# Weight pieces in an attention and expert kernel: spread over sixteen groups, with low parts made on VectorE

## The chip, the cores and the metric

The kernel runs on one core of one Trainium2 chip. A core has a matrix engine (TensorE, PE in the profile, with its weight loads as PEld), a vector engine (VectorE, DVE), an activation engine (ScalarE, ACT), GpSimd (POOL) and SyncE (SP), which here only starts DMAs. Each engine works through its own list of instructions in order and waits on semaphores that others raise. The metric is the time of one execution in microseconds (us), as the median of several runs.

## The reference

```python
def reference(x, wq, bq, wk, bk, wv, bv, wo, bo, Ws, bs, Wg, Wu, Wd):   # x: (8, 512, 256) float16
    # attention: 16 heads of 16, causal, on the normalised rows
    n = layernorm(x)
    q, k, v = (n @ wq.T + bq) * 0.25, n @ wk.T + bk, n @ wv.T + bv      # split into heads
    attn = softmax(q k^T + causal mask).astype(float16)
    x = x + layernorm((attn v) @ wo.T + bo)
    # experts: 8 of them, 688 wide, the two best for each row
    n = layernorm(x)
    top, idx = top_k(n @ Ws + bs, 2);  combine = one_hot(idx) * softmax(top)
    h = silu(n Wg[e]) * (n Wu[e]);     y = h Wd[e]                      # Wg, Wu, Wd in float32
    return x + layernorm(sum over e of combine[e] * y[e])
```

## The kernel before

The attention part walks over 8 batches, and in each over 4 groups of 4 heads: 32 groups, numbered 0 to 31 (a group's number modulo 4 is its place in its batch, g). A group is 12 fills (i = 0 to 11). In each fill TensorE computes a block of transposed scores of this group (L1417) and, beside it in other rows of the array, a block of plain scores of the group after next (L1408). VectorE takes the row maxima of the plain ones (`maxima`, L1035), ScalarE exponentiates the transposed ones (L894, which writes pT), and GpSimd zeroes what lies above the diagonal (`cut`, an affine select, L681). TensorE then multiplies with the values (L1448). TensorE may start the scores of fill i when ScalarE has exponentiated up to fill i-2, and the plain scores of fill i when VectorE has taken the maxima up to fill i-2, since each has two banks. All other work is placed by hand at a fill: projections, the norms (`next_norm` for the next batch at g = 0, `finish` for the batch before at g = 1 and 2), the routing of rows (`route`, `slots` at g = 3) and the scatter of rows for the experts. The norm's root is GpSimd's: `rsqrt` is four small instructions, two of them powers of about 1 us each.

From group 18 on (FIRST_TILE) tiles of the expert part are woven into the groups; a later part (from about 712 us) does the other tiles and a last norm.

The expert weights are float32 in memory and are used as two float16 parts. There are 24 pieces (8 experts, Wg, Wd and Wu of each; n % 3 == 1 is Wd). A piece n is loaded by SyncE into one of two stages (`load_piece`), when the low part of piece n-2 is done, which frees its stage. Then, before the change:

- `high_part(n)` on ScalarE (L820): high = float16(256 * stage),
- `scale_stage(n)` on ScalarE (L826): stage = 256 * stage, in place,
- `low_part(n)` on GpSimd (L668): low = stage - high.

Pieces 0 to 5 (EARLY = 6) go through ahead of group 0; after them each of groups 0 to 8 has two (PIECES_AT), at fills 3 and 4 and at fills 7 and 8 of ScalarE's order and behind the first and second `cut` of GpSimd's.

At the start GpSimd writes all constants (L615 to L650) and raises const_ready, and only then comes `rsqrt(0)`, on which the first normalised rows `xn` wait. TensorE waits for const_ready ahead of its first transposition, VectorE ahead of its first bias of the values. SyncE clears the 8 MB of `expert_rows` with one DMA at the end of batch 2's list (L564). The pieces' DMAs and all others of SyncE are issued in the order of its code, each behind the waits of those ahead of it.

## Time and profile before

| | us |
|---|---|
| median of 3 runs (lowest, highest) | 924.04 (924.03, 924.41) |
| the profiled execution, its own time | 925.53 |
| its span, first to last instruction | 923.4 |
| groups 0 to 31 of the attention part | 49.42 to 620.53 |
| busy: PE, DVE, ACT, POOL | 769.0, 629.2, 556.9, 471.1 |
| mean granted TensorE clock | 0.79 |

The profile is of one execution. In a table of stretches the numbers are the stretch, its length, and for each engine its busy time in it with the count of its instructions, then the granted clock of TensorE (1.00 is 2.4 GHz, 0.50 is 1.2 GHz), the share of the DMA engines and the rate. In a timeline a row is the start, the duration, the engine, the line, the operation, what it writes and reads, and in brackets how long the engine had been idle and what released it. Group boundaries are taken at the first exponential (L894) of each group.

### The profile page before, as it was taken

To read this page: it belongs to the slowest core of one execution; us is meant where nothing else is said; L and a number is where in the kernel's file an instruction comes from. 1 tells how busy PE (TensorE), PEld (TensorE's weight loads), DVE (VectorE), ACT (ScalarE), POOL (GpSimd) and SP (SyncE) were. 2 spreads that over 40 slices of the span, in tenths; PEclk is the share of its full clock that TensorE was granted. 3 is DMA by queue.
4 is the path that set the end of the run, shared out by engine and by line. 5 is a ranking of instruction groups with operands and counts; after the bars stand their busy time and mean duration, and the time that the engine had idled before them with its cause. 6 is when DMAs were issued, how large, how long until landed. Compare 5 with 4: busy or idle time off the path is not lost. (4 is left out here: it accounts for less than half of the span.)

```text
span 923.4 us, 21865 instructions
## 1 busy us (share of the span) xinstructions
PE 769.0 (83%) x6606; PEld 447.4 (48%) x6607; DVE 629.2 (68%) x2328; ACT 556.9 (60%) x1101; POOL 471.1 (51%) x540
## 2 busy tenths in 40 slices
PE   3568886789999999988998899898977999999930
PEld 1122232333333335554554455466865878778720
DVE  3855668778877787888889787755644555555546
ACT  3589887675666567665676577555543444444427
POOL 3575647475352445675366447757544223333227
PEclk9555555555555569998999899899997999999975
DMA  5343323315601011122111212212333532323248
GB/s 173 126 121 98 120 77 112 91 38 187 223 24 30 25 41 16 22 48 53 19 30 31 41 19 43 53 25 45 56 73 84 110 41 40 46 34 47 34 104 283
DMA packets 69243, 66.52 MB, mean 72 GB/s; under 512 B 5536, under 2 KB 62752, under 8 KB 69152
## 3 DMA queue, kind: packets, MB, share of 16 engines
q1 hardware_dynamic: 55872, 50.86, 17.9%
q0 software_dynamic: 13280, 14.49, 11.2%
q8 instruction: 51, 0.84, 0.4%
q14 instruction: 40, 0.33, 0.1%
HBM read 34.04 MB, written 31.29 MB: 71 GB/s over the span
## 5 line engine op out<-in xcount | busy, mean ns | idle before, releaser
L1035 DVE CUSTOM_DVE_ANT_0 unused<-bank,mask 128x384 f16<-128x384 f32 (+3 forms) x512 | 235.9, 485 | 83.8 <-PE bank L1408 80.7
L894 ACT ACTIVATE pT<-bank 128x512 f16<-128x512 f32 (+1 forms) x384 | 201.7, 533 | 108.9 <-PE bank L1417 105.8
L1417 PE MATMUL bank<-qT,kT 32*128 32x384 f16 (+3 forms) x512 | 176.3, 390 | 29.3 <-ACT pT L894 27.4
L1408 PE MATMUL bank<-kT,qT 32*128 32x384 f16 (+3 forms) x512 | 178.6, 398 | 8.2 <-DVE nmax L1035 7.7
L681 POOL TENSOR_SCALAR_AFFINE_SELECT pT<-pT 128x512 f16<-128x512 f16 x128 | 84.7, 706 | 129.1 <-ACT pT L894 128.4
L1837 POOL DMA_INDIRECT expert_rows<-y_sb,dest x36 | 56.0, 1555 | 118.8 <-DVE y_sb L1956 113.3
L1510 PE MATMUL bank<-tile_xT,gu_part 128*128 128x256 f16 (+1 forms) x616 | 90.0, 287 | 11.7 <-DVE stage L1219 11.6
L2031 PE MATMUL bank<-xT,gu_part 128*128 128x256 f16 (+1 forms) x792 | 94.7, 277 | 2.4 <-issue 1.4
L1417 PEld LDWEIGHTS bank<-qT,kT 32*128 32x128 f16 x512 | 39.5, 97 | 117.3 <-issue 60.6
L1448 PEld LDWEIGHTS bank<-va,pT 128*128 128x128 f16 x1280 | 49.4, 102 | 91.6 <-issue 66.7
L2031 PEld LDWEIGHTS bank<-xT,gu_part 128*128 (+1 forms) x792 | 77.9, 101 | 18.0 <-issue 3.7
L1448 PE MATMUL bank<-va,pT 128*128 128x17 f16 x1280 | 70.1, 176 | 15.5 <-POOL pT L681 15.3
L160 POOL DMA_INDIRECT dispatch_rows<-rows,slot x64 | 65.3, 1021 | 21.3 <-issue 16.6
L2056 PE MATMUL bank<-wd_part,h 128*128 (+2 forms) x612 | 75.4, 273 | 0.6 <-ACT h L1878 0.3
L1510 PEld LDWEIGHTS bank<-tile_xT,gu_part 128*128 (+1 forms) x616 | 58.2, 103 | 28.1 <-issue 17.6
L1528 PE MATMUL bank<-wd_part,stage 128*128 (+2 forms) x476 | 70.7, 283 | 0.3 <-DVE stage L1225 0.3
L707 POOL DMA_INDIRECT expert_rows<-tile_y,tile_dest x34 | 54.8, 1613 | 26.1 <-ACT tile_y L879 19.9
L1871 ACT ACTIVATE act_g<-bank 128x512 f32<-128x512 f32 (+1 forms) x72 | 32.5, 477 | 55.2 <-PE bank L2031 55.2
L668 POOL TENSOR_TENSOR gu_part<-stage,gu_part 128x1280 f16<-128x1280 f32 (+1 forms) x32 | 47.0, 1488 | 35.5 <-ACT stage L826 35.5
L2056 PEld LDWEIGHTS bank<-wd_part,h 128*128 128x128 f16 (+2 forms) x612 | 54.0, 97 | 17.5 <-issue 10.9
L1878 ACT ACTIVATE h<-hid 128x512 f16<-128x512 f32 (+1 forms) x72 | 37.7, 523 | 40.9 <-DVE hid L1936 40.2
L1936 DVE SCALAR_TENSOR_TENSOR hid<-bank,act_g 128x512 f32<-128x512 f32 (+1 forms) x72 | 39.9, 554 | 31.3 <-ACT act_g L1871 30.7
(198 smaller groups left out, 1439.7 us busy)
## 6 DMA issues: line engine op xcount, KB each, us to landing
expert_rows<-tile_in SPq DMA_DIRECT2D x1, 8192.0 KB, 26.5
stage<-wg SPq DMA_DIRECT2D x8, 688.0 KB, 4.1
stage<-wu SPq DMA_DIRECT2D x8, 688.0 KB, 4.1
stage<-wd SPq DMA_DIRECT2D x8, 640.0 KB, 4.1
gu_part<-expert_rows SPq DMA_DIRECT2D x16, 256.0 KB, 6.5
out<-gu_part SPq DMA_DIRECT2D x16, 256.0 KB, 2.5
tile_in<-dispatch_rows SPq DMA_DIRECT2D x21, 130.0 KB
rows<-dispatch_rows SPq DMA_DIRECT2D x18, 130.0 KB
```

The lines of the kernel that those rows point to most:

```text
L160: gp.indirect_dma_start(out=xs_dram[:, :], in_=keep["rows"][:, t, r, :], in_offset=None, out_offset=bass.IndirectOffsetOnAxis(ap=keep["slo ...
L681: last = gp.affine_select(out=diagonal, in_=diagonal, compare_op=ALU.is_ge, fill=0.0, base=0, pattern=[[0, J], [1, P]], channel_multiplier=-1)
L894: sc.activation(pT[:, lo:hi], ST_BANK[i % 2][:, 0:hi - lo], ACT.Exp, scale=1.0 / INV_SCALE).then_inc(p_ready, 1)
L1035: last = v.tensor_tensor_reduce(out=unused[:, i % 2, at:at + n], in0=S_BANK[i % 2][:, at:at + n], in1=mask[:, T - n:T], scale=-1.0, scalar ...
L1408: last = mm(S_BANK[i % 2][:, at:at + n], qT[32 * j:32 * j + 32, g, P * qt:P * (qt + 1)], kT[32 * j:32 * j + 32, g, 0:n], start=True, stop= ...
L1417: last = mm(ST_BANK[i % 2][:, at:at + n], kT[32 * j:32 * j + 32, g, P * kt:P * (kt + 1)], qT[32 * j:32 * j + 32, g, P * kt:T], start=True, ...
L1448: last = mm(OUT[:, qt, j, 0:HD + 1], pT[:, at:at + P], va[:, g, kt, j, :], start=(i == 0 and qt == 0), stop=(i == NF - 1 and qt == QT - 1))
L1510: last = mm(target, keep["gu"][part][:, bass.ds(col + (k * GU + at), width_)], tile_xT[n % 2][:, k, :], start=(s == 0), stop=(s == 2 * KD ...
L1528: last = mm(Y_BANK[:, D * t:D * (t + 1)], h[0:rows, c // 2, at:at + P], keep["wd"][w][0:rows, bass.ds(col + c * D, D)], start=(c == 0 and ...
L1837: gp.indirect_dma_start(out=ys_dram[:, :], in_=y_sb[j][:, t, :], in_offset=None, out_offset=bass.IndirectOffsetOnAxis(ap=dest[j][:, t:t + ...
L2031: last = mm(dst[0:width, :], gu_part[part][:, bass.ds(col + (k * GU + at), width)], xT[j][:, k, :], start=(s == 0), stop=(s == 2 * KD - 1))
L2056: last = mm(Y_BANK[t][:, 0:D], h[0:rows, c // 2, at:at + P], wd_part[w][0:rows, bass.ds(col + c * D, D)], start=(c == 0 and s == 0), stop= ...
```

## The change

It does six things.

1. EARLY is 5: pieces 0 to 4 go through ahead of group 0. Groups 0 to 3 have two pieces each, groups 4 to 13 and group 15 one each (group 14 none): PIECES_OF.
2. Pieces 0 to 4 and the first piece of each of groups 0 to 3 keep the old way (POOLED, nine pieces). The other 15 have no `scale_stage` and no `low_part` on GpSimd. VectorE makes their low part straight from the unscaled stage, low = 256 * stage - high, as a scalar_tensor_tensor in two halves (`low_half`): at fills 10 and 11 in groups 0 to 3, later at the fills of LOW_AT. The high part is at fill 7 in groups 0 to 3, later at HIGH_AT.
3. The semaphore lo_ready becomes two, pool_low and dve_low, and a load waits for the one that its stage's last piece raises.
4. GpSimd's constants are put in another order: what `rsqrt(0)` and the first transposition need comes first, then `rsqrt(0)`, then the rest and const_ready. TensorE waits for the new ident_ready ahead of the transposition, and for const_ready ahead of its first projection.
5. The clear of `expert_rows` is eight DMAs, one in each of groups 8 to 15 of SyncE's list. The first tile's load and store wait for all eight.
6. SyncE's loads of pieces are spread like the pieces: each group's list holds the loads of its pieces' successors but one.

```diff
-        EARLY = 6
-        PIECES_AT = {(b, g): tuple(range(EARLY + 2 * (G * b + g), min(EARLY + 2 * (G * b + g) + 2, PIECES)))
-                     for b in range(B) for g in range(G)}
+        EARLY = 5
+        PIECES_OF = [2] * G + [1] * (2 * G) + [1, 1, 0, 1]
+        LAST_PIECES = len(PIECES_OF)
...
+        POOLED = tuple(range(EARLY)) + tuple(PIECES_AT[0, g][0] for g in range(G))
+        LOW_RANK = [sum((m in POOLED) == (n in POOLED) for m in range(n)) for n in range(PIECES)]
+        HIGH_AT = (6, 0, 5, 6)
+        LOW_AT = ((8, 9), (2, 3), (7, 8), (8, 9))
+        CLEARS = 2 * G
...
-                        sp.wait_ge(lo_ready, n - 1)
+                        sp.wait_ge(pool_low if n - 2 in POOLED else dve_low, LOW_RANK[n - 2] + 1)
...
+                    def pieces(g):
+                        for n in PIECES_AT[b, g]:
+                            if n + 2 < PIECES:
+                                load_piece(n + 2)
+
+                    def clear_rows(g):
+                        n = G * b + g - 2 * G
+                        if 0 <= n < CLEARS:
+                            rows = RESULTS // CLEARS
+                            sp.wait_ge(const_ready, 1)
+                            sp.dma_start(ys_dram[n * rows:(n + 1) * rows, :].rearrange("(n p) d -> p n d", p=P),
+                                         clear.unsqueeze(1).broadcast_to([P, rows // P, D])
+                                         ).then_inc(keep["cleared"], 16)
...
                 def low_part(n):
 
-                    pool.wait_ge(scaled_ready, n + 1)
+                    pool.wait_ge(scaled_ready, LOW_RANK[n] + 1)
...
-                            if c < len(PIECES_AT[b, g]):
-                                low_part(PIECES_AT[b, g][c])
+                            if first and c == 0:
+                                low_part(PIECES_AT[b, g][0])
...
-                            if i in (3, 7) and i // 4 < len(PIECES_AT[b, g]):
+                            if first and i in (3, 7):
                                 high_part(PIECES_AT[b, g][i // 4])
-                            if i in (4, 8) and i // 4 <= len(PIECES_AT[b, g]):
-                                scale_stage(PIECES_AT[b, g][i // 4 - 1])
+                            if first and i == 4:
+                                scale_stage(PIECES_AT[b, g][0])
+                            if not first and i == HIGH_AT[g]:
+                                for n in PIECES_AT[b, g]:
+                                    high_part(n)
...
+                def low_half(n, half):
+
+                    if half == 0:
+                        dve.wait_ge(hi_ready, n + 1)
+                    for (dst, src), (high, _) in zip(places(n, 1), places(n, 0)):
+                        if n % 3 == 1:
+                            cols = slice(half * FC * D // 2, (half + 1) * FC * D // 2)
+                            last = v.scalar_tensor_tensor(dst[:, cols], src[:, cols], WSCALE, high[:, cols], ALU.mult, ALU.subtract)
+                        else:
+                            last = v.scalar_tensor_tensor(dst[:, half, :], src[:, half, :], WSCALE, high[:, half, :],
+                                                          ALU.mult, ALU.subtract)
+                    if half:
+                        last.then_inc(dve_low, 1)
...
+                            if i in ((10, 11) if first else LOW_AT[g]):
+                                for m in PIECES_AT[b, g][1:] if first else PIECES_AT[b, g]:
+                                    low_half(m, i - (10 if first else LOW_AT[g][0]))
...
-                pe.wait_ge(const_ready, 1)
+                pe.wait_ge(ident_ready, 1)
                 pe.wait_ge(xn_ready, 1)
                 transpose4(("xnT", 0), xn, range(KD))
                 pe.wait_ge(w_in, 16 * 10)
+                pe.wait_ge(const_ready, 1)
```

**Place 1: GpSimd, from the constants to the first norm.** The rows give the line, the operation and the tile. Before:

```order
L632 IOTA iota_s 128x4
L634 MEMSET gu_part 128x16x16 x2
L636 MEMSET ident 128x128
L637 AFFINE_SELECT ident<-ident 128x128
L640 MEMSET before 128x128
L641 AFFINE_SELECT before<-before 128x128
L644 MEMSET mask 128x512
L646 AFFINE_SELECT mask<-mask 128x128
L649 MEMSET va 128x16 x4
L657 TENSOR_SCALAR veps<-mv 128x4
```

With the change:

```order
L656 MEMSET gu_part 128x16x16 x2
L658 MEMSET before 128x128
L659 AFFINE_SELECT before<-before 128x128
L634 TENSOR_SCALAR veps<-mv 128x4
L635 CAST mean<-mv 128x4
L637 TENSOR_TENSOR std<-veps,power 128x4
L639 TENSOR_TENSOR rstd<-std,power 128x4
L662 IOTA iota 128x8
L664 IOTA fill 128x8
L666 IOTA next 128x9
L668 MEMSET one_early 128x8
```

The norm's four instructions (veps to rstd) stand ahead of six small constants, the mask and the four columns of va; ident has moved ahead of spare_ids.

**Place 2: ScalarE, a group of batch 1.** L820 (L836 in the change) is `high_part`, L826 (L842) is `scale_stage`, L894 (L911) the exponentials. Before, from fill 3 on:

```order
L799 ACTIVATE qT<-bank,bq_sb 128x512
L820 ACTIVATE gu_part<-stage 128x2x640
L820 ACTIVATE gu_part<-stage 128x2x48
L894 ACTIVATE pT<-bank 128x512
L826 ACTIVATE stage<-stage 128x1376
L894 ACTIVATE pT<-bank 128x512
L802 ACTIVATE kT<-bank,bk_sb 128x512
L894 ACTIVATE pT<-bank 128x512 x2
L807 ACTIVATE v<-bank 128x256
L820 ACTIVATE wd_part<-stage 128x1536
L894 ACTIVATE pT<-bank 128x256
L809 ACTIVATE qT<-bank 128x512
```

With the change, the same stretch of group 4:

```order
L815 ACTIVATE qT<-bank,bq_sb 128x512
L911 ACTIVATE pT<-bank 128x512 x2
L818 ACTIVATE kT<-bank,bk_sb 128x512
L911 ACTIVATE pT<-bank 128x512
L836 ACTIVATE wd_part<-stage 128x1536
L911 ACTIVATE pT<-bank 128x512
L823 ACTIVATE v<-bank 128x256
L911 ACTIVATE pT<-bank 128x256
L825 ACTIVATE qT<-bank 128x512
```

One high part stands where two high parts and two scalings stood.

**Place 3: VectorE, the end of a group at g = 3 (group 11).** L1035 (L1055 in the change) is `maxima`, L1128 (L1148) and after it `slots`, L1257 is `low_half`. Before:

```order
L1035 ISA unused,nmax<-bank,mask 128x512
L1035 ISA nmax 128x1
L1025 TENSOR_TENSOR va<-v,bv_sb 128x16x16
L1035 ISA unused,nmax<-bank,mask 128x512
L1035 ISA nmax 128x1
L1035 ISA unused,nmax<-bank,mask 128x512
L1035 ISA nmax 128x1
L1128 TENSOR_TENSOR row<-bank,fill 128x32
```

With the change:

```order
L1055 ISA unused,nmax<-bank,mask 128x512
L1055 ISA nmax 128x1
L1257 SCALAR_TENSOR_TENSOR gu_part<-stage,gu_part 128x640
L1257 SCALAR_TENSOR_TENSOR gu_part<-stage,gu_part 128x48
L1045 TENSOR_TENSOR va<-v,bv_sb 128x16x16
L1055 ISA unused,nmax<-bank,mask 128x512
L1055 ISA nmax 128x1
L1257 SCALAR_TENSOR_TENSOR gu_part<-stage,gu_part 128x640
L1257 SCALAR_TENSOR_TENSOR gu_part<-stage,gu_part 128x48
L1055 ISA unused,nmax<-bank,mask 128x512
L1055 ISA nmax 128x1
L1148 TENSOR_TENSOR row<-bank,fill 128x32
```

The two halves of a low part stand behind the maxima of fills 8 and 9, ahead of `slots`.

## Rows read from the trace of the kernel before

**Rows 1.** The page's second part: granted TensorE clock in 40 equal slices.

```profile
PEclk9555555555555569998999899899997999999975
```

**Rows 2.** Table of stretches: groups 4 to 12.

```profile
109.64:126.97 17.33, 14.47 (x111) 5.80 (x112) 13.39 (x48) 14.44 (x25) 12.69 (x14) 0.50 0.28 87
126.97:143.57 16.60, 13.41 (x97) 4.75 (x94) 10.42 (x44) 13.74 (x25) 7.84 (x9) 0.50 0.33 102
143.57:164.56 20.99, 13.17 (x100) 4.95 (x100) 18.09 (x52) 12.77 (x21) 13.76 (x14) 0.50 0.33 100
164.56:180.61 16.05, 13.31 (x130) 5.28 (x131) 11.08 (x56) 14.33 (x25) 6.52 (x6) 0.50 0.27 88
180.61:200.04 19.43, 15.85 (x111) 6.08 (x112) 16.53 (x59) 14.61 (x23) 12.95 (x14) 0.50 0.17 50
200.04:213.37 13.33, 13.21 (x97) 4.74 (x94) 9.98 (x44) 8.96 (x20) 10.29 (x15) 0.50 0.10 32
213.37:228.23 14.86, 13.03 (x101) 5.14 (x100) 12.66 (x52) 8.12 (x17) 7.56 (x12) 0.50 0.67 223
228.23:241.51 13.28, 12.97 (x131) 5.28 (x130) 9.81 (x56) 9.74 (x20) 2.38 (x4) 0.50 1.05 348
241.51:258.19 16.68, 15.78 (x111) 6.07 (x111) 12.64 (x60) 9.86 (x19) 7.59 (x12) 0.50 0.29 95
```

**Rows 3.** Timeline, all engines: from GpSimd's constants to the first projection.

```profile
3.00 0.14 POOL L624 IOTA iota<- 128x8 f32 x1 [0.24 <-POOL ids L622]
...
4.80 0.31 POOL L634 MEMSET gu_part<- 128x256 f16 x1 [0.15 <-POOL iota_s L632]
...
5.67 0.38 DVE L1007 BATCH_NORM_AGGREGATE mv<-stats 128x2 f16<-128x6 f32 x4
...
7.50 0.53 POOL L644 MEMSET mask<- 128x512 f16 x1 [0.16 <-POOL before L641]
...
9.75 0.24 POOL L657 TENSOR_SCALAR veps<-mv 128x4 f16<-128x4 f16 x1
...
12.37 1.11 DVE L1015 TENSOR_SCALAR xn<-x_sb,mean,rstd 128x256 f16<-128x256 f16 x4 [6.32 <-POOL rstd L662]
...
15.91 1.01 PE L1390 MATMUL bank<-xnT,wq_sb 128*128 128x512 f16 x2 [1.27 <-ACT xnT L795]
```

**Rows 4.** Timeline of ScalarE: the last piece ahead of group 0.

```profile
46.70 1.43 ACT L820 ACTIVATE gu_part<-stage 128x1280 f16<-128x1280 f32 x2
...
49.42 1.07 ACT L894 ACTIVATE pT<-bank 128x512 f16<-128x512 f32 x2
```

**Rows 5.** Timelines of VectorE and GpSimd: three places where both work at once.

```profile
60.04 1.24 POOL L681 TENSOR_SCALAR_AFFINE_SELECT pT<-pT 128x512 f16<-128x512 f16 x2
...
60.72 0.70 DVE L1025 TENSOR_TENSOR va<-v,bv_sb 128x256 f16<-128x256 f16 x1
...
190.35 3.25 DVE L1015 TENSOR_SCALAR xn<-x_sb,mean,rstd 128x256 f16<-128x256 f16 x1
190.41 3.10 POOL L668 TENSOR_TENSOR wd_part<-stage,wd_part 128x1536 f16<-128x1536 f32 x1 [0.67 <-ACT stage L826]
...
222.04 1.04 POOL L660 TENSOR_TENSOR std<-veps,power 128x4 f16<-128x4 f16 x1
...
222.61 0.29 DVE L1025 TENSOR_TENSOR va<-v,bv_sb 128x256 f16<-128x256 f16 x1
```

**Rows 6.** Timeline of TensorE: two waits for ScalarE, in groups 0 and 2.

```profile
55.89 0.50 PE L1417 MATMUL bank<-qT,kT 32*128 32x384 f16 x1 [1.46 <-ACT pT L894]
...
93.25 0.39 PE L1417 MATMUL bank<-qT,kT 32*128 32x256 f16 x1 [1.08 <-ACT pT L894]
```

**Rows 7.** Groups by line and shape: VectorE's subtractions in the later part (count, busy us, mean ns).

```profile
L1943 DVE TENSOR_TENSOR h<-hid,h 128x512 f16<-128x512 f32 x36 | 25.2, 701 | 25.7 <-ACT h L1878 24.9 <-issue 0.8
...
L1943 DVE TENSOR_TENSOR h<-hid,h 128x256 f16<-128x256 f32 x18 | 7.7, 426 | 0.5
```

**Rows 8.** Table of stretches: from slots in group 11 to fill 6 of group 12.

```profile
241.10:250.20 9.10, 8.81 (x48) 2.58 (x46) 8.66 (x48) 5.15 (x9) 3.53 (x6) 0.50 0.43 142
```

79 lines of the change are left out of this document (41 added, 38 removed).

## The prediction

> **What bounds the kernel now.** I read the granted clock first, then a table of stretches cut at the groups, then timelines inside the groups, and last the prices by shape.
>
> TensorE runs at half its clock, 1.2 GHz, in 13 of the first 14 slices of the page and at about full clock afterwards [rows 1]. In that slow stretch two kinds of group stand side by side. Groups 9 to 12 have no weight piece: TensorE is busy in 13.21 of 13.33 us, 12.97 of 13.28, 15.78 of 16.68 [rows 2]. They are bound by TensorE at its low clock. Groups 4 to 8 have two pieces each and take 17.33, 16.60, 20.99, 16.05 and 19.43 us, though TensorE's work in them is the same within 0.3 us at the same place g, but for group 4 [rows 2]. Their idle TensorE time is 2.9, 3.2, 7.8, 2.7 and 3.6 us: that is what the pieces cost. Two mechanisms make it. First, ScalarE: its high parts and scalings stand between exponentials, and TensorE waits for those, as in the 1.46 us in group 0 and the 1.08 us in group 2 [rows 6]. The same 1.08 recurs in groups 1 and 3. Second, GpSimd's subtraction holds VectorE: a tensor_scalar of VectorE that began 0.06 us ahead of a 3.10 us subtraction took 3.25 us [rows 5] and ended with it. Behind it queue the row maxima, and behind those TensorE. From group 12 on nothing of the pieces is left in the trace. The end follows from there through the tiles, so time won in groups 0 to 16 is won in full, unless something new is late.
>
> **The start.** The moments of the first norm are ready at 6.05 (5.67 + 0.38), but GpSimd starts the root at 9.75, behind its constants [rows 3]. The change moves two stretches of constants behind it: 3.00 to 4.80, and 7.50 to 9.75, 4.05 us in all. The root can't start before the moments, and ids, which VectorE waits for in its first memsets, comes a little later (two more instructions ahead of it). So it starts at about 6.25, 3.5 us earlier. The first projection follows xn by 15.91 - 12.37 = 3.5 us [rows 3] and would start at about 12.4. But it now waits for const_ready. The root takes 2.5 us (9.75 to about 12.3), to 8.8, and the 4.05 us of constants behind it end at about 12.9. I take 2.9 us won; the ends are 0 (the pieces' loads don't follow) and 3.5.
>
> With EARLY = 5 the high part and scaling of piece 5 no longer stand ahead of the first exponential: 49.42 - 46.70 = 2.7 us [rows 4]. ScalarE is the last to arrive there, so all of it is won. Together **5.6 us**.
>
> **Groups 0 to 3.** Each keeps two high parts and one scaling on ScalarE and loses the scaling at fill 8. The 1.08 us wait behind that scaling [rows 6] goes, four times: 4.3. In group 0 piece 5's data is loaded earlier than piece 6's was, and most of the 1.46 goes: 1.2. Against it VectorE gets two halves at fills 10 and 11 in a stretch where it is idle about half the time; I take 0.7 for the four groups. One subtraction a group stays on GpSimd, and it will still meet the norm of group 0. **4.8 us** won.
>
> **Groups 4 to 8.** Without any piece I expect the busy time of TensorE in the group plus the idle time of the clean group at the same g: 14.47 + 0.9 = 15.4 for group 4, 13.5 for 5, 13.17 + 1.8 = 15.0 for 6, 13.6 for 7, and 16.7 for 8, the length of group 12 [rows 2]. That is 74.2 against 90.4 us: **16.2 us** won. One high part of about 1.4 us per group stays on ScalarE. It is free: ScalarE was idle in 3.5 to 6.8 us of the groups without pieces (13.28 - 9.74, 16.68 - 9.86) [rows 2], and GpSimd has no subtraction left there.
>
> **The price of the low parts on VectorE.** No such instruction is in the trace. The nearest is the float32 subtraction from SBUF: 426 ns for 256 columns and 701 for 512 [rows 7], so 1.07 ns a column and 0.15 fixed. A half of 640 + 48 columns occupies about 0.8 us, one of 768 about 0.9. 15 pieces make 24.8 us. The part on the path has the ends 0 and 24.8. VectorE is idle for 3.4, 2.2, 3.5 and 4.0 us in groups 9 to 12 [rows 2], more than 1.65 each time, so I take the value by what stands behind each place:
> - g = 3 (groups 7, 11; 15 likewise): two halves ahead of slots. From slots to fill 6 of the next group VectorE is busy 8.66 of 9.10 us [rows 8]. Only about 0.4 us of idle lies ahead, so 1.2 us go on to the next group, three times: 3.6.
> - g = 2 (groups 6, 10): they push the second norm's scaling at fills 9 and 10, which was itself waiting for the root: 0.5 each, 1.0.
> - g = 1 (groups 5, 9, 13): VectorE waits for TensorE at fills 0 to 3; 0.2, 0.2 and, with the plan behind it, 0.4: 0.8.
> - g = 0 (groups 4, 8, 12): the halves fall where VectorE is idle again: 0.
> - meetings with GpSimd's selects: a two-input add took 0.70 us beside a select, and 0.29 beside the root's power [rows 5]. So only the selects count, 0.4 to 0.6 a meeting. By their places few meet; I take 1.5 in all.
>
> **6.9 us** lost.
>
> Here a rule of the Trainium skill speaks against the change. Its page SBUF — State Buffer, section Who interferes with whom, says that a VectorE instruction with two SBUF inputs contends with a GpSimd instruction that reads SBUF, and whichever is second blocks until the first is done. `low_half` is such an instruction. For the select and the subtraction the trace agrees, for the power it does not. By the rule a half could be held by any GpSimd work beside it; that is the second rival.
>
> **The rest.** The clear in one piece filled the DMA engines in group 11 (share 1.05), and the group took the same 13.28 us that TensorE needs [rows 2]. Eight clears of an eighth cost nothing on this evidence, with or against; a late load would be their only harm, and each piece is now loaded over a group ahead. The two semaphores cost nothing.
>
> Sum: 5.6 + 4.8 + 16.2 - 6.9 = 19.7 us. The profiled execution took 925.53 and would take 905.8; it stands 1.5 above the median, so the median goes from 924.04 to **904.3**.
>
> **Rivals.**
> - *The start gives only the piece.* The loads of pieces 2 and 4 each wait for a low part of GpSimd and then for the transfer, and ScalarE waits for them ahead of group 0. If that chain doesn't shift with xn, 2.9 us are lost again: 907.2. Against it: each link of it begins with a release by ScalarE, whose work follows xn. 10%.
> - *Slower: VectorE and GpSimd hold each other.* If every one of the 30 halves meets a select of 0.62 us and nothing of the low parts is hidden, the price is 24.8 + 30 x 0.62 = 43.4 instead of 6.9 us, and the kernel takes 940.8. It decides from a price of 26.6 / 15 = 1.77 us a piece on the path, more than the whole instruction pair, so only with the meetings. For it: [rows 5]. Against: VectorE's idle time of 2.2 to 4.0 us a group, and the powers and scatters don't hold it. 3%.
> - *VectorE becomes the bound.* All 24.8 on the path, with few meetings: 904.3 + 17.9 = 922.2. It would need VectorE without idle time in each group. 5%.
> - *The clock rises earlier.* TensorE without its gaps in groups 4 to 8 could be granted full clock there. VectorE would then bound these groups at its busy 10 to 13 us plus the low parts, where I count 13.3 to 17.9: some 30 us more over 14 groups, about 874. Against it: groups 9 and 11 kept TensorE busy 98 to 99% and stayed at 0.50 [rows 2]. The skill's page TensorE: Matmul & The Clock Gate, Part 1, says that activity releases the throttle; by that alone the rise could come earlier, but these rows show a busy engine that isn't released. 4%.
>
> **How the numbers follow.** The forecast has 78%. Its bounds: the start 0 to 3.5, the low parts 3 to 14, groups 0 to 8 by 3 us either way, and the clock's changes after group 17, which may fall differently by 2 us or so. That gives 895 to 912, and it holds the first rival. With the other three at 12% that range should hold the time 8 times in 10. A measurement of this kernel can tell about 0.2%, 1.8 us, from no change. Faster by more: 96% (the forecast, the first and fourth rival and most of the third); within 0.2%: 1%; slower: 3%.
>
> **What would show it.** Right: the first xn at about 8.9 and the first exponential of group 0 near 43.8; groups 1 to 3 near 14; 4 to 7 at 15.4, 13.7, 15.5 and 13.6, and 8, 12 and 16 near 17.9; half of a Wg piece near 0.7 us for its 640 columns; the clock at 0.5 until about 8 us into group 18. Wrong: VectorE instructions of over 1.2 us beside selects; groups 9 to 16 each over a microsecond longer; waits of TensorE for row maxima in most fills; ScalarE waiting for stage loads after group 0; or a tile that waits for the clears in group 16.

## Result: 9.3 us faster, a little under half of what was forecast

| | before | changed |
|---|---|---|
| median of 4 runs on one chip, us | 924.22 (924.03 to 924.48) | 914.95 (913.95 to 915.81) |
| ratio | | 0.9896 (95%: 0.9869 to 0.9923) |
| profiled execution, its own time | 925.53 | 913.95 |
| its span | 923.4 | 912.2 |
| first exponential of group 0 | 49.42 | 44.16 |
| groups 0 to 17 | 283.78 | 275.84 |
| groups 18 to 31 | 287.34 | 291.91 |
| behind group 31 | 302.84 | 300.27 |

The forecast was 904.3 with a range up to 912. Between the two spans lie 11.2 us, against 19.7 forecast. Up to group 18 the profile shows 13.2; the groups behind it took 4.6 more and the later part 2.6 less. The medians are 9.3 us apart and not 11.6, as the two profiled times are, because the profiled execution stands 1.3 us above its median before the change and 1.0 below with it; no stage explains that part.

The ratios below leave out executions that took over 1.5% longer than the fastest of their kernel (912.95 and 1232.26 us with the halves in VectorE's gaps, 940.14 us with the small subtractions, 940.51 us of before), and the profiles of 912.95 and 940.14 us are used up to group 17 only, where the granted clock is 0.50 as in all traces.

The page of the changed kernel, granted TensorE clock in 40 slices, answers to [rows 1]. There too 13 of the first 14 slices are at half clock:

```profile
PEclk9555555555555579988998899799997999999975
```

The start, from the timeline of all engines, answers to [rows 3]. GpSimd's root no longer waits behind the constants, and xn comes 3.2 us earlier (12.37 to 9.15):

```profile
6.90 1.05 POOL L637 TENSOR_TENSOR std<-veps,power 128x4 f16<-128x4 f16 x1
...
9.15 1.11 DVE L1035 TENSOR_SCALAR xn<-x_sb,mean,rstd 128x256 f16<-128x256 f16 x4 [2.70 <-POOL rstd L639]
...
13.31 1.01 PE L1428 MATMUL bank<-xnT,wq_sb 128*128 128x512 f16 x2 [1.89 <-POOL va L676]
...
41.25 1.48 ACT L836 ACTIVATE wd_part<-stage 128x1536 f16<-128x1536 f32 x1 [5.71 <-DMA stage<-wd]
```

The table of stretches, groups 2 to 6, 8, 11 and 12 of the changed kernel (columns as in [rows 2]):

```profile
71.95:86.86 14.91, 13.07 (x92) 4.38 (x92) 10.19 (x40) 11.40 (x20) 5.64 (x7) 0.50 0.39 125
86.86:101.33 14.47, 13.02 (x93) 4.38 (x92) 9.79 (x38) 11.36 (x22) 5.79 (x7) 0.50 0.26 87
101.33:118.98 17.65, 15.85 (x111) 6.09 (x111) 14.27 (x55) 11.11 (x19) 5.19 (x9) 0.50 0.23 65
118.98:132.61 13.63, 13.63 (x96) 5.05 (x94) 11.90 (x48) 10.10 (x21) 4.57 (x8) 0.50 0.37 120
132.61:148.27 15.66, 13.00 (x100) 5.08 (x101) 14.26 (x56) 9.12 (x18) 5.97 (x9) 0.50 0.25 80
162.48:180.43 17.95, 16.43 (x113) 6.33 (x114) 14.30 (x69) 11.09 (x21) 7.62 (x11) 0.50 0.18 54
209.88:224.03 14.15, 13.39 (x125) 5.24 (x124) 11.23 (x54) 10.75 (x22) 3.30 (x4) 0.50 0.16 56
224.03:242.39 18.36, 16.42 (x113) 6.32 (x114) 14.69 (x69) 11.07 (x20) 7.48 (x11) 0.50 0.37 118
```

Groups 5, 6 and 8 are where the forecast put them (13.7, 15.5, 17.9). Group 4 is not: 17.65 us against 15.4. Nor are 2 and 3, forecast near 14. TensorE's idle time did fall in these, to 1.8, 1.5 and 1.8 us; but it is *busy* longer, 15.85 us in group 4 against 14.47 in [rows 2], with 111 instructions in both. The next section takes this apart.

### The profile page after: what moved, and what is told of

It is laid out like the page before. It is cut to its first block and busy times, and to the rows that moved or that the text cites. A ratio compares the mean times of both kernels' runs of the same rounds, so it can differ in the third digit from the quotient of the medians.

```text
span 912.2 us, 21884 instructions
## 1 busy us (share of the span) xinstructions
PE 778.4 (85%) x6606; PEld 451.9 (50%) x6607; DVE 640.6 (70%) x2378; ACT 538.2 (59%) x1086; POOL 435.6 (48%) x515
## 5 line engine op out<-in xcount | busy, mean ns | idle before, releaser
L1055 DVE CUSTOM_DVE_ANT_0 unused<-bank,mask 128x384 f16<-128x384 f32 (+3 forms) x512 | 235.2, 484 | 61.1 <-PE bank L1446 58.1
L911 ACT ACTIVATE pT<-bank 128x512 f16<-128x512 f32 (+1 forms) x384 | 202.0, 531 | 122.5 <-PE bank L1455 121.2
L1455 PE MATMUL bank<-qT,kT 32*128 32x384 f16 (+3 forms) x512 | 177.6, 393 | 14.1 <-ACT pT L911 13.0
L1446 PE MATMUL bank<-kT,qT 32*128 32x384 f16 (+3 forms) x512 | 179.0, 399 | 9.5 <-DVE nmax L1055 8.8
L698 POOL TENSOR_SCALAR_AFFINE_SELECT pT<-pT 128x512 f16<-128x512 f16 x128 | 88.3, 734 | 170.5 <-ACT pT L911 170.3
L1548 PE MATMUL bank<-tile_xT,gu_part 128*128 128x256 f16 (+1 forms) x616 | 94.0, 297 | 6.9 <-DVE stage L1239 6.6
L1455 PEld LDWEIGHTS bank<-qT,kT 32*128 32x128 f16 x512 | 39.5, 97 | 103.1 <-issue 60.2
L160 POOL DMA_INDIRECT dispatch_rows<-rows,slot x64 | 66.8, 1043 | 21.3 <-issue 16.7
L1566 PE MATMUL bank<-wd_part,stage 128*128 (+2 forms) x476 | 72.7, 289 | 0.0
L1548 PEld LDWEIGHTS bank<-tile_xT,gu_part 128*128 (+1 forms) x616 | 60.3, 107 | 22.7 <-issue 11.7
L1231 DVE SCALAR_TENSOR_TENSOR stage<-stage,bank 128x256 f32<-128x256 f32 x84 | 34.9, 416 | 39.7 <-ACT stage L869 38.8
L869 ACT ACTIVATE stage<-bank 128x256 f32<-128x256 f32 x84 | 32.2, 383 | 50.9 <-PE bank L1548 50.4
```

The costliest lines, as they stand in the source:

```text
L160: gp.indirect_dma_start(out=xs_dram[:, :], in_=keep["rows"][:, t, r, :], in_offset=None, out_offset=bass.IndirectOffsetOnAxis(ap=keep["slo ...
L698: last = gp.affine_select(out=diagonal, in_=diagonal, compare_op=ALU.is_ge, fill=0.0, base=0, pattern=[[0, J], [1, P]], channel_multiplier=-1)
L911: sc.activation(pT[:, lo:hi], ST_BANK[i % 2][:, 0:hi - lo], ACT.Exp, scale=1.0 / INV_SCALE).then_inc(p_ready, 1)
L1055: last = v.tensor_tensor_reduce(out=unused[:, i % 2, at:at + n], in0=S_BANK[i % 2][:, at:at + n], in1=mask[:, T - n:T], scale=-1.0, scalar ...
L1446: last = mm(S_BANK[i % 2][:, at:at + n], qT[32 * j:32 * j + 32, g, P * qt:P * (qt + 1)], kT[32 * j:32 * j + 32, g, 0:n], start=True, stop= ...
L1455: last = mm(ST_BANK[i % 2][:, at:at + n], kT[32 * j:32 * j + 32, g, P * kt:P * (kt + 1)], qT[32 * j:32 * j + 32, g, P * kt:T], start=True, ...
```

## Experiments

The chips of these runs differed: the kernel before took 931.21, 925.45, 932.45 and 933.03 us there, with runs from 922.3 to 940.5, where the forecast's chip had 924.22. So the times in microseconds that the expectations name, made for that chip, can't be held against these runs within some us: each kernel is compared by its ratio to before, and by the length of its groups 0 to 17 in the trace. That sum repeats well: 275.84, 275.76 and 275.92 us in three traces of the changed kernel, 283.78, 283.74 and 283.97 in three of before. Every row but the first keeps the changed kernel's start, with EARLY = 5 (the last has 4), and so has 19 pieces in groups 0 to 17 (the last 20), where before had 18.

| groups, us | 0-3 | 4-8 | 9-17 | 0-17 | ratio to before |
|---|---|---|---|---|---|
| before | 60.22 | 90.40 | 133.16 | 283.78 | 1 |
| changed | 57.17 | 79.10 | 139.57 | 275.84 | 0.990 |
| no halves | 54.64 | 74.71 | 133.80 | 263.15 | 0.971 |
| all lows on GpSimd | 59.10 | 82.54 | 144.85 | 286.48 | 0.999 |
| two a group | 57.19 | 92.04 | 135.03 | 284.26 | 0.994 |
| halves in gaps | 57.13 | 76.80 | 133.91 | 267.84 | 0.973 |
| first piece | 55.33 | 77.45 | 139.61 | 272.39 | 0.982 |
| both placements | 55.39 | 75.19 | 133.92 | 264.50 | 0.972 |
| both, EARLY = 4 | 60.08 | 75.17 | 134.41 | 269.66 | 0.968 |

### What the halves cost

```diff
-                        sp.wait_ge(pool_low if n - 2 in POOLED else dve_low, LOW_RANK[n - 2] + 1)
+                        if n - 2 in POOLED:
+                            sp.wait_ge(pool_low, LOW_RANK[n - 2] + 1)
+                        else:
+                            sp.wait_ge(hi_ready, n - 1)
...
+                            if n not in POOLED:
+                                sp.wait_ge(hi_ready, n + 1)
+                                for (dst, _), (high, _) in zip(places(n, 1), places(n, 0)):
+                                    sp.dma_start(dst, high).then_inc(dve_low, 16)
...
-                            if i in ((10, 11) if first else LOW_AT[g]):
-                                for m in PIECES_AT[b, g][1:] if first else PIECES_AT[b, g]:
-                                    low_half(m, i - (10 if first else LOW_AT[g][0]))
```

> The changed kernel without VectorE's halves; the 15 low parts are left out (a DMA puts a copy of the high part in their place). Theory A, the halves make the row maxima late and so pull TensorE's pairs of plain and transposed scores apart: groups 2, 3 and 4 become shorter by about 1.0, 1.0 and 1.7 us, groups 9 to 16 by the 6.4 us that they lost against the kernel before, the pairs overlap for 5.5 us a group again, and the kernel takes 901 to 903 us. Rival B, VectorE is late in groups 0 to 8 with or without the halves, once ScalarE no longer holds TensorE back: only groups 9 to 16 become shorter, 908 to 909 us. Rival C, the halves are hidden and the loss is made elsewhere: 914 to 916 us.

Measured: 902.46 us, ratio 0.9707 (0.9652 to 0.9761). Groups 0 to 17 take 263.15 us, 12.7 less than with the halves. Theory A holds, B and C fall. Groups 2, 3 and 4 became shorter by 1.41, 1.01 and 1.62 us. The edit also frees a stage at the high part, earlier than the changed kernel can. That this isn't the gain is shown by the run of both placements below: it makes every low part and takes 264.50 us over the same groups.

The timeline shows how a late VectorE costs time without a wait of TensorE that one would see. First the changed kernel, TensorE and VectorE at the start of group 3 (86.86): L1455 is the transposed scores, L1446 the plain ones, L1255 a half, L1055 the maxima.

```profile
85.88 0.95 DVE L1255 SCALAR_TENSOR_TENSOR wd_part<-stage,wd_part 128x768 f16<-128x768 f32 x1
86.22 0.60 PE L1455 MATMUL bank<-qT,kT 32*128 32x512 f16 x1
86.22 0.60 PE L1446 MATMUL bank<-kT,qT 32*128 32x384 f16 x2
86.75 0.68 DVE L1055 CUSTOM_DVE_ANT_0 unused<-bank,mask 128x512 f16<-128x512 f32 x1
86.97 0.60 PE L1455 MATMUL bank<-qT,kT 32*128 32x512 f16 x1
87.36 0.09 DVE L1055 DVE_READ_ACCUMULATOR2_ANT nmax<- 128x1 f16 x1
87.36 0.95 DVE L1255 SCALAR_TENSOR_TENSOR wd_part<-stage,wd_part 128x768 f16<-128x768 f32 x1
87.50 0.60 PE L1446 MATMUL bank<-kT,qT 32*128 32x384 f16 x2
```

Then the same place without the halves (L1460 transposed, L1451 plain, L1063 maxima):

```profile
85.07 0.60 PE L1460 MATMUL bank<-qT,kT 32*128 32x512 f16 x1
85.08 0.60 PE L1451 MATMUL bank<-kT,qT 32*128 32x384 f16 x2
...
85.82 0.60 PE L1460 MATMUL bank<-qT,kT 32*128 32x512 f16 x1
85.83 0.60 PE L1451 MATMUL bank<-kT,qT 32*128 32x384 f16 x2
85.86 0.56 DVE L1063 CUSTOM_DVE_ANT_0 unused<-bank,mask 128x384 f16<-128x384 f32 x1 [0.19 <-PE bank L1451]
```

The plain and the transposed scores work in different rows of the array and run side by side: both start at 86.22 and both take 0.60. With the half ahead of it the row maximum is read out at 87.36 only, and the next plain scores start at 87.50 where the transposed ones started at 86.97. The two now run one behind the other, 0.53 us lost, and TensorE shows as busy throughout. (The starts are recorded; the ends of matmuls are modelled by the profile.) That is why, from before to the changed kernel, TensorE's idle time in group 3 fell by 1.4 us (2.86 to 1.45) and the group's length only by 0.5: 0.9 went into busy time. In groups 2, 3 and 4 the two kinds overlap for 4.44, 4.49 and 3.88 us, against 5.49, 5.49 and 5.47 before and 5.49, 5.49 and 5.11 without the halves (the time in which both run, summed over the trace of the group).

The price by kind, VectorE's groups by shape in the changed kernel (count, busy us, mean ns):

```profile
L1257 DVE SCALAR_TENSOR_TENSOR gu_part<-stage,gu_part 128x640 f16<-128x640 f32 x20 | 17.8, 889 | 0.0
L1255 DVE SCALAR_TENSOR_TENSOR wd_part<-stage,wd_part 128x768 f16<-128x768 f32 x10 | 10.3, 1029 | 0.0
L1257 DVE SCALAR_TENSOR_TENSOR gu_part<-stage,gu_part 128x48 f16<-128x48 f32 x20 | 6.6, 329 | 0.0
```

That is 34.7 us, 2.3 a piece, where the forecast had 24.8. Of the 50 instructions, 38 were not held and took 0.95 us (768 columns), 0.82 (640) and 0.20 (48), which makes 29.9 us for all. The other 4.8 are holds: 12 instructions took 0.3 to 0.4 us longer, each beside a select of GpSimd. Here two instructions take 1.36 us from 124.07, beside a select that began at 124.00:

```profile
124.00 0.64 POOL L698 TENSOR_SCALAR_AFFINE_SELECT pT<-pT 128x512 f16<-128x512 f16 x1 [5.71 <-ACT pT L911]
124.07 1.36 DVE L1257 SCALAR_TENSOR_TENSOR gu_part<-stage,gu_part 128x640 f16<-128x640 f32 x2
```

Halves beside GpSimd's casts, powers and scatters were not held. It can be GpSimd that waits: the cast of the norm's mean, 0.18 us elsewhere, took 0.83 beside a half, while that half and the one beside the powers took, with their 48 columns, 0.94, as with nothing beside them:

```profile
141.06 0.94 DVE L1257 SCALAR_TENSOR_TENSOR gu_part<-stage,gu_part 128x640 f16<-128x640 f32 x2
141.10 0.83 POOL L635 CAST mean<-mv 128x4 f32<-128x4 f16 x1
141.90 1.04 POOL L637 TENSOR_TENSOR std<-veps,power 128x4 f16<-128x4 f16 x1
142.53 0.94 DVE L1257 SCALAR_TENSOR_TENSOR gu_part<-stage,gu_part 128x640 f16<-128x640 f32 x2
```

### Spreading and VectorE, one at a time

The first edit spreads the pieces but leaves every low part to GpSimd, the second gives the halves to VectorE but doesn't spread.

```diff
-        POOLED = tuple(range(EARLY)) + tuple(PIECES_AT[0, g][0] for g in range(G))
+        POOLED = tuple(range(PIECES))
...
-                            if first and c == 0:
-                                low_part(PIECES_AT[b, g][0])
+                            if first and c < 2:
+                                low_part(PIECES_AT[b, g][c])
+                            elif not first and c == 1:
+                                for n in PIECES_AT[b, g]:
+                                    low_part(n)
...
+                            if not first and i == HIGH_AT[g] + 1:
+                                for n in PIECES_AT[b, g]:
+                                    scale_stage(n)
```

> The spreading of the changed kernel alone: one piece a group from group 4 on, as before the change with a scaling on ScalarE and a subtraction on GpSimd. Theory A, the gain comes from taking the scaling and the GpSimd subtraction away, which cost about 1.6 us a piece (16.2 us for the ten pieces of groups 4 to 8): 15 pieces x 1.6 in place of about 13 us for the halves, so about 11 us slower than the changed kernel, 925 to 927 us. Rival, the spreading makes the gain, and one piece a group hides whichever engine does it: 905 to 915 us.

```diff
-        PIECES_OF = [2] * G + [1] * (2 * G) + [1, 1, 0, 1]
+        PIECES_OF = [2] * (2 * G + 1) + [1]
```

> VectorE's halves without the spreading: groups 4 to 8 have two pieces each and group 9 one, both pieces at the fills of the changed kernel. Theory A, a piece costs about 0.85 us wherever it is: groups 4 to 9 cost 4.7 us more than with one piece, groups 10 to 17 4.7 less, the sum of groups 0 to 17 is 275 to 277 and the kernel takes 914 to 916. Rival, two pieces are more than VectorE has idle time for in a group (4 us of halves against 1.5 to 4.5 us) and two high parts more than ScalarE's pace allows: groups 4 to 8 take 8 to 12 us more, the sum is 279 to 283 and the time 918 to 922.

Spreading alone: 928.36 us, ratio 0.9988 (0.9954 to 1.0021), groups 0 to 17 at 286.48, 2.7 more than before. VectorE alone: 925.76 us, ratio 0.9940 (0.9914 to 0.9965), 284.26 us, 0.5 more than before. Together they give 275.84. So theory A of the first run holds (10.6 us more than the changed kernel), and that of the second falls; its rival has the direction, but groups 4 to 8 took 12.9 us more, beyond its 8 to 12. Neither half of the change gains anything in these groups by itself, though both versions bring one piece more into them than before had; the two make 7.9 us together. With two pieces in a group the halves crowd, and ScalarE comes to wait for loads, as its waits in groups 4 to 8 show (us in total, times, longest):

```profile
ACT gu_part L836 <- DMA stage<-wg: 2.2, 1, 2.2
ACT wd_part L836 <- DMA stage<-wd: 2.0, 1, 2.0
```

How much of the 8.4 us is crowding and how much the fills, which were chosen for one piece, this run doesn't tell.

### How GpSimd holds VectorE

The run with all low parts on GpSimd, each subtraction cut into instructions of 128 columns.

```diff
-                        last = gp.tensor_tensor(dst, src, high, ALU.subtract)
+                        if n % 3 == 1:
+                            for c in range(0, FC * D, D // 2):
+                                last = gp.tensor_tensor(dst[:, c:c + D // 2], src[:, c:c + D // 2], high[:, c:c + D // 2], ALU.subtract)
+                        else:
+                            size = src.shape[-1]
+                            step = P if size > P else size
+                            for k in range(KD):
+                                for c in range(0, size, step):
+                                    last = gp.tensor_tensor(dst[:, k, c:c + step], src[:, k, c:c + step], high[:, k, c:c + step],
+                                                            ALU.subtract)
```

> The run with all low parts on GpSimd, one piece a group, with each subtraction cut into instructions of 128 columns instead of 640 to 1536 (some 12 a piece). Theory A, VectorE is held for the length of one GpSimd instruction: no VectorE instruction takes more than about 1 us beside them, group 6 goes from 19.25 to about 16.5 us and group 10 from 19.74 to about 16.5, in all 6 to 8 us less than with whole subtractions, 918 to 921 us. Rival, VectorE is held for the whole work however it is cut: groups 6 and 10 stay above 19 us and the time at 924 to 930.

Measured: 926.35 us, ratio 1.0002 (0.9978 to 1.0026); groups 6 and 10 take 18.86 and 18.91 us against 19.25 and 19.74, and groups 0 to 3 take 64.65 against 59.10. The mechanism of theory A is there, its gain is not: groups 4 to 17 take 4.2 us less than with whole subtractions, and groups 0 to 3 take 5.6 more. Timelines of group 10, first with whole subtractions:

```profile
212.27 3.65 DVE L1040 TENSOR_SCALAR rows<-y,mean,rstd 128x256 f16<-128x256 f16 x2
212.75 3.09 POOL L685 TENSOR_TENSOR wd_part<-stage,wd_part 128x1536 f16<-128x1536 f32 x1
```

and with small ones:

```profile
219.81 0.99 DVE L1049 TENSOR_SCALAR rows<-y,mean,rstd 128x256 f16<-128x256 f16 x2
220.29 4.66 POOL L687 TENSOR_TENSOR wd_part<-stage,wd_part 128x128 f16<-128x128 f32 x12
...
221.34 1.00 DVE L1049 TENSOR_SCALAR rows<-y,mean,rstd 128x256 f16<-128x256 f16 x2
```

Two scalings beside the subtraction took 3.65 us and take 0.99: VectorE waits for one instruction of GpSimd, not for its work. This is the lock that the Trainium skill describes on its page SBUF — State Buffer, section Who interferes with whom, held for a whole instruction, and the trace agrees. But the work grew from 3.09 us to 4.66, and from 2.93 to 4.36 for a Wg or Wu piece, and now the select behind it is late. TensorE waits for that in the same group:

```profile
205.05 4.36 POOL L693 TENSOR_TENSOR gu_part<-stage,gu_part 128x128 f16<-128x128 f32 x12
209.35 0.65 POOL L707 TENSOR_SCALAR_AFFINE_SELECT pT<-pT 128x512 f16<-128x512 f16 x1
...
210.06 0.27 PE L1496 MATMUL bank<-va,pT 128*128 128x17 f16 x4 [3.17 <-POOL pT L707]
```

### The start and the clears

```diff
-                pool.sem_inc(ident_ready, 1)
...
-                rsqrt(0)
...
                 last.then_inc(const_ready, 1)
+                rsqrt(0)
...
-                pe.wait_ge(ident_ready, 1)
```

(The cut lines move ident, gu_part and before behind iota_s again.)

> The changed kernel with GpSimd's constants and the first root in the order of before, and TensorE waiting for const_ready alone. Theory A: the first xn comes about 3 us later and the first exponential with it, at 46.7 to 47.0 instead of 44.16; 917.5 to 918.5 us. Rival, the loads of the pieces set the first exponential and don't follow xn: it stays at 44.2 and the time at 914 to 916.

Measured: 920.88 us, ratio 0.9897 (0.9867 to 0.9927). xn is 3.2 us later (12.36 against 9.15), the first exponential 2.1 us (46.28 against 44.16), groups 0 to 17 the same (275.88). So of the 5.3 us won at the start the constants make 2.1 and the rest, 3.1, is put down to the piece, which no run took away alone; a third of what xn gains doesn't reach the first exponential. The first exponential itself differs by 0.8 us between executions (43.8 to 44.6 in eleven traces whose code up to there is the changed kernel's), so the 2.1 are good to half a microsecond or so, and the 3.2 of xn to 0.03. The ratio, with its wide interval, can't show 2 us on this chip; the trace can.

```diff
-        CLEARS = 2 * G
+        CLEARS = 1
...
-                        n = G * b + g - 2 * G
+                        n = G * b + g - 3 * G + 1
```

> The changed kernel with the clear in one DMA of 8 MB at the end of batch 2's list, as before. Theory A, the eight parts bring nothing: groups 0 to 17 take 275.8 us within 0.3 and the kernel 912 to 916. Rival, the one clear delays the loads behind it now that they are one a group: groups 11 to 13 become 1 us or more longer, 916 to 918.

Measured: 914.93 us, ratio 0.9842 (0.9781 to 0.9903), groups 0 to 17 at 275.83, each group within 0.01. The eight parts bring nothing.

### Where a half is free

```diff
-                            if i in ((10, 11) if first else LOW_AT[g]):
+                            if i in ((9, 10) if first else LOW_AT[g]):
                                 for m in PIECES_AT[b, g][1:] if first else PIECES_AT[b, g]:
-                                    low_half(m, i - (10 if first else LOW_AT[g][0]))
+                                    low_half(m, i - (9 if first else LOW_AT[g][0]))
```

> In groups 0 to 3 the halves stand behind the maxima of fills 9 and 10, not 10 and 11. Theory A, it is the place next to the following group's first fills, where VectorE has no idle time left, that pulls the pairs apart: at most one pair is lost in groups 2, 3 and 4, each is 0.5 to 1 us shorter, 912.5 to 913.5 us. Rival, the half costs its 0.95 us wherever it stands: 914.5 to 915.5 us, with the late pairs at other fills.

Measured: 915.12 us, ratio 0.9850 (0.9788 to 0.9913). Groups 0 to 4 sum to 74.83 us in both: group 4 gave back 0.5, group 1 took 0.7. Theory A in this form falls: one fill earlier there is no more room. The run without halves shows where there is. VectorE in its group 4, the wait behind fill 7:

```profile
109.96 0.69 DVE L1063 CUSTOM_DVE_ANT_0 unused<-bank,mask 128x512 f16<-128x512 f32 x1 [2.49 <-PE bank L1451]
```

The changed kernel has its halves of that group behind fills 8 and 9, just past the gap. (There they turned out to cost nothing either: a table further down has the count by place.) Two runs use the gaps, one from group 4 on, one in groups 0 to 3:

```diff
-        HIGH_AT = (6, 0, 5, 6)
-        LOW_AT = ((8, 9), (2, 3), (7, 8), (8, 9))
+        HIGH_AT = (5, 0, 5, None)
+        LOW_AT = ((7, 7), (2, 2), (11, 11), (1, 1))
...
+                            if not first and (g, i) == (2, 9):
+                                for n in PIECES_AT[b, 3]:
+                                    high_part(n)
```

> The changed kernel with the halves of groups 4 to 15 put where VectorE waits in the run without halves: both behind fill 7 at g = 0 (gap of 2.5 us there), both behind fill 2 at g = 1 (1.26 and 0.40), both behind fill 11 at g = 2 (1.21), both behind fill 1 at g = 3 (1.36 and 0.31), with the high parts a fill or more ahead. Theory A, a half costs what of it does not fit into the gap behind its maxima: by those gaps 0, 0.3, 0.7 and 0.4 us a piece instead of 0.8 to 1.0, groups 5 to 17 take about 4.5 us less than in the changed kernel, 910 to 911 us. Rival, a half costs some 0.4 us wherever it stands in a group: no change, 914 to 916. Other rival, two halves in a row hold the maxima longer than one and cost more: 916 to 919.

```diff
-        POOLED = tuple(range(EARLY)) + tuple(PIECES_AT[0, g][0] for g in range(G))
+        POOLED = tuple(range(EARLY)) + tuple(PIECES_AT[0, g][1] for g in range(G))
...
-                            if first and c == 0:
-                                low_part(PIECES_AT[b, g][0])
+                            if first and c == 1:
+                                low_part(PIECES_AT[b, g][1])
...
-                            if i in ((10, 11) if first else LOW_AT[g]):
+                            if i in ((5, 6) if first else LOW_AT[g]):
```

> In groups 0 to 3 VectorE makes the low part of the first piece, behind the maxima of fills 5 and 6 (gaps of 1.0 and 1.4 us in the run without halves), and GpSimd that of the second, with its scaling at fill 8. Theory A: the pairs of plain and transposed scores stay together in groups 2 to 4 (2.5 us less in groups 0 to 3, 1 to 1.6 in group 4), but the wait behind the scaling at fill 8, 1.08 us a group, is back: the sum of groups 0 to 4, 74.8 us in the changed kernel, becomes 74 to 76. Rival, the halves are no cause of the separated pairs: they stay, and the sum is 78 to 79.

The gaps: 897.65 and 906.08 us, ratio 0.9733 (0.9665 to 0.9801) by these two executions; the reading rests on the trace, where groups 5 to 17 take 193.1 us against 201.0, 7.9 less, and each is within 0.05 us of the run without halves, but for groups 7 and 11 (0.49 each) and group 17. Theory A holds, and more was to be had than it said. The first piece: 910.28 us, ratio 0.9823 (0.9788 to 0.9858); groups 0 to 4 take 71.36 us against 74.83, below the 74 to 76 of its theory. Group 4, whose own halves stayed at fills 8 and 9, takes 16.03 us, as without any halves (16.04). The 1.08 us behind the scaling at fill 8 did not come back in full: groups 2 and 3 are 0.6 us above the run without halves.

Both together, and then with one piece fewer ahead of group 0:

> The two better placements together: in groups 0 to 3 VectorE's halves for the first piece at fills 5 and 6 and GpSimd for the second, from group 4 on the halves in VectorE's gaps. If the gains of the two runs that made them one at a time (3.5 us by the first, 8.0 by the second, each in its own groups) add up, groups 0 to 17 take 264.4 us instead of 275.8 and the kernel 902 to 905 us, within 1.5 us of the run without any halves over these groups (263.15). If one uses up the idle time that the other needs, as at the border of groups 3 and 4, 267 to 269 us for the groups and 906 to 908.

```diff
-        EARLY = 5
-        PIECES_OF = [2] * G + [1] * (2 * G) + [1, 1, 0, 1]
+        EARLY = 4
+        PIECES_OF = [2] * G + [1] * (3 * G)
```

> The two placements, and one piece fewer ahead of group 0 (EARLY = 4), with a piece in group 14. Theory A, the last piece ahead of group 0 costs its load (ScalarE waits 5.7 us for it in the changed kernel) and 2.9 us on ScalarE: the first exponential comes at about 36 instead of 44.2, groups 0 to 17 take 264.5 to 266 us, and the kernel 894 to 897. Rival, the load is only late at another place, in group 0 or 1: the first exponential at 36 but groups 0 to 3 up to 6 us longer, 899 to 902.

Both: 905.45 us (902.46 to 907.82), ratio 0.9723 (0.9672 to 0.9773), groups 0 to 17 at 264.50 as the sum said. With EARLY = 4: **901.91 us** (899.27 to 903.13), ratio 0.9678 (0.9630 to 0.9727), the lowest ratio here; on the same chip it took 3.5 us less than the run of both. Its first exponential comes at 36.15, 8.2 us earlier, but group 0 takes 18.57 us instead of 13.87, and groups 0 to 17 take 269.66, beyond theory A's 266. The rival's size is right (groups 0 to 3 took 4.7 us longer than with EARLY = 5), but neither theory had the reason: in group 0 ScalarE waits for no load, and TensorE waits for VectorE's maxima for 3.6 us. From the timeline of all engines there:

```profile
35.58 2.61 POOL L685 TENSOR_TENSOR gu_part<-stage,gu_part 128x1280 f16<-128x1280 f32 x1 [0.42 <-ACT stage L842]
...
36.53 1.69 DVE L1327 CAST ws_part<-ws_f 128x16 bf16<-128x16 f32 x1
...
40.62 0.60 PE L1451 MATMUL bank<-kT,qT 32*128 32x384 f16 x2 [2.27 <-DVE nmax L1058]
...
42.33 0.60 ACT L911 ACTIVATE pT<-bank 128x512 f16<-128x512 f32 x1 [3.34 <-PE bank L1460]
```

VectorE has the maxima of groups 0 and 1 and then three casts and two subtractions of 16 columns to do ahead of its first batch, and the first cast is held until the subtraction of GpSimd ends. That this makes group 0 longer is read from the trace; no run moved the casts.

### What the clock does behind group 17

The same kernels once more, unchanged:

> The changed kernel once more. If the clock's low stretches behind group 17 hang on the program, groups 18 to 31 take 291.9 us again with low stretches at the same places; if they fall differently from one execution to the next, the groups up to 17 take the same within 0.1 us each and groups 18 to 31 some 288 to 294.

> The kernel before, unchanged. If groups 18 to 31 took 4.6 us less in its first trace than in the changed kernel's by the chance of the clock, they take 288 to 294 us here, as in the ten traces with the change's code there, while groups 0 to 17 take 283.8 us again. If the program sets it (its tiles start at another place of the attention part's time), they take 287.3 within 1 us again.

> The kernel before once more, for the spread between two executions in a row: groups 0 to 17 at 283.8 us; groups 18 to 31 at 288 to 294 us if chance, at 287.3 within 1 us if the program sets it.

> The changed kernel a third time, on the same chip as the two runs of before: groups 0 to 17 at 275.8 us; groups 18 to 31 in the same range as before's (288 to 294) if chance, 291.9 if the program sets it.

The changed kernel took 912.59 us (ratio 0.9862, 0.9819 to 0.9904) in the first of these runs. The single runs took 926.61 and 932.91 (before) and 915.43 (changed). Groups 18 to 31 of six traces, in the order before, twice before again, changed, twice changed again (columns as in [rows 2]; the granted clock is the third number from the end):

```profile
333.19:620.53 287.34, 258.30 (x2549) 153.71 (x2549) 231.37 (x893) 188.51 (x416) 170.53 (x212) 0.94 0.19 34
...
333.78:621.18 287.40, 256.52 (x2549) 153.80 (x2549) 230.70 (x892) 188.44 (x416) 170.45 (x212) 0.95 0.19 34
...
334.20:627.76 293.56, 263.55 (x2549) 156.21 (x2549) 230.99 (x893) 189.30 (x416) 171.64 (x212) 0.92 0.18 34
...
319.99:611.90 291.91, 265.13 (x2549) 156.91 (x2549) 230.78 (x893) 189.57 (x416) 172.24 (x213) 0.91 0.19 34
...
319.75:608.67 288.92, 260.93 (x2549) 154.45 (x2549) 229.99 (x893) 189.61 (x416) 173.38 (x213) 0.93 0.19 34
```

(The sixth took 290.28.) Before gives 287.3 to 293.6, the changed kernel 288.9 to 291.9, the same work each time. The longer ones have the lower mean clock, 0.91 and 0.92 against 0.94 and 0.95. So the 4.6 us are within what one execution differs from the next, and are not shown to come from the change. Nor is chance shown: of the two repeats of before one took 293.56, as expected by chance, and the other 287.40, as expected if the program sets it, and two of the three traces of before lie below all others with the change's code (288.9 and up). Three traces a kernel don't decide it. Behind group 31 it is alike: 302.8, 303.3 and 303.0 us before, and 300.3, 299.5 and 302.8 changed, so the 2.6 us won there are not shown to come from the change either. Why the clock's short low stretches fall where they do stays open.

On the chip of the forecast the changed kernel's ratio is 0.9896; when it was taken again, on another chip, it is 0.9862, and on a third it is 0.9842 for the kernel with one clear, whose groups up to 17 are the same. So the change is worth 9 us on the first chip and by these ratios some 13 to 15 us on two others, nearer to the 13.2 that the traces show up to group 18; but the intervals of all three overlap.

## Why the forecast missed, by its own steps

| step | forecast | measured in the traces |
|---|---|---|
| the start | +5.6 | +5.3 (2.1 constants, the rest the piece) |
| groups 0 to 3 without the halves' 0.7 | +5.5 | +5.6 (60.22 - 54.64) |
| groups 4 to 8 without the halves | +16.2 | +15.7 (90.40 - 74.71) |
| groups 9 to 17 | 0 | -0.6 (133.16 - 133.80) |
| the halves on VectorE | -7.6 (0.7 + 6.9) | -12.7 (4.15 + 8.54 = 275.84 - 263.15) |
| groups 18 to 31, and behind | 0 | -4.6, +2.6 |
| sum, by the spans | +19.7 | +11.2 |

**The start** was right in its mechanism and its size: xn at 9.15 (forecast 8.9), the first exponential at 44.16 (43.8). The first rival, that the chain ahead of the first exponential doesn't follow xn, is true for 1.1 of the 3.2 us; in the trace ScalarE waits 5.71 us for a load there. What is left for the piece is 0.4 more than 2.7.

**Removing the GpSimd subtractions and the scalings** was right to half a microsecond, by reading the groups without pieces beside those with two.

**The price of the halves** is the step that failed, 5.1 of the 8.5 us missed. It went wrong in two places.

In groups 0 to 3 I took 0.7 us because VectorE "is idle about half the time". Groups 1 to 4 lost 0.1, 1.4, 1.0 and 1.6 us to these four pieces, 4.1 in all. (Group 4's 1.6 are of the halves that end group 3: with those moved, and its own left where they are, it takes 16.03 us.) The share was about true (VectorE was busy in 34.8 of 60.2 us before) and said nothing: the two halves stand behind fills 10 and 11, next to the 512-wide fills that open the next group, and the idle time lies behind fills 5 and 6, where the run of the first piece put them.

The other eleven pieces cost 8.5 us instead of 6.9. By place, against the run without halves:

| halves at | forecast | measured |
|---|---|---|
| g = 3 (groups 7, 11, 15, and what they pass to 8, 12, 16) | 3.6 | 5.1 |
| g = 2 (groups 6, 10) | 1.0 | 1.8 |
| g = 1 (groups 5, 9, 13, and 14) | 0.8 | 2.1 |
| g = 0 (groups 4, 8, 12) | 0 | 0 |
| meetings with selects | 1.5 | in the rows above |
| group 17 | | -0.4 |

The three zeros of g = 0 were right. Groups 8, 12 and 16 are 0.53, 0.95 and 0.94 us longer than without halves, but all of that is there by their third exponential, before their own halves at fills 8 and 9, and group 16 has no piece at all. It is what g = 3 passes on. Group 16, changed and without halves:

```profile
287.83:305.44 17.61, 16.42 (x113) 6.32 (x114) 13.43 (x66) 9.85 (x18) 7.46 (x11) 0.50 0.08 24
...
276.06:292.74 16.68, 15.78 (x111) 6.09 (x112) 12.65 (x60) 9.85 (x18) 7.59 (x12) 0.50 0.22 70
```

Under this price lies a slip in the sum. The forecast read 1.07 ns a column and 0.15 us fixed from [rows 7] and then took 0.9 us for 768 columns and 0.8 for 640 + 48. By its own figures these are 0.97 and, in two instructions, 1.04, and 30.4 us for all instead of 24.8. The traces have 0.95 and 1.02. At g = 3 that alone makes 2.0 us a piece instead of 1.65, of which with the same 0.4 us of idle time 1.6 and not 1.2 are passed on, 4.8 for the three; 5.1 were measured. And 12 instructions met a select, 4.8 us of holds, where 1.5 was taken for the path; how much of the 4.8 lies on the path isn't shown.

**Group 4** was forecast at 15.4 us and takes 16.04 without halves. The base was its own busy time of before, 14.47, which was the time with all its pairs side by side. I had noted that group 4 stands apart from group 8 and did not ask why: at 15.85 and 15.78 groups 8 and 12 have three pairs apart already before the change.

**The high part is free** is true but for g = 0: groups 8 and 12 without halves take 17.42 us, and group 12 takes 16.68 where it has no piece (before, and with two a group). So group 8 met its forecast of 17.9 by luck: 16.7 + 1.2 was expected, and it is 16.7, 0.7 for the high part and 0.5 from group 7.

**The rivals.** VectorE did not become the bound, and the mutual hold stayed small. The second rival had any GpSimd work beside a half hold it; in the trace only selects did, and powers, casts and scatters didn't. Of the two places in [rows 5] that the forecast called agreeing, the one of the subtraction isn't clear: the instruction held there has one tensor as input and began 0.06 us ahead. The clock did not rise earlier: group 5 kept TensorE busy in 13.63 of 13.63 us and stayed at 0.50. Its rise fell in group 18 in every trace. The range allowed 3 to 14 us for the low parts and so held the 12.7. But with 12.7 in place of 7.6 the time is 909.4, and the rest came out worse too: 1.4 us in the start and the groups up to 17, 2.0 behind group 17, and some 2.1 by where the profiled executions stand to the medians. The range had no room for all of these together. The last two terms lie within what executions differ by, and may as well be chance.

## What to carry to other kernels

When work moves to an engine with "enough idle time", find the gap that each instruction will stand in: the low part of a piece cost 1.5 to 1.8 us behind fills 8 and 9 of a group at g = 3, 0.05 behind fill 1 of it (groups 15 and 16), and nothing behind fills 8 and 9 of a group at g = 0. And redo the price of an instruction from the fixed part and the slope that you read, once for each instruction. The busy time of a TensorE whose matmuls run side by side is no fixed amount: check whether pairs that overlap in one group still do in the other before taking a group's busy time as its floor. And test the parts of a combined change apart: here each of two parts alone gained nothing in these groups, and a third did nothing that could be seen.
